# Two chains of a two-layer transformer block on one core: other places for their vector steps

## The reference, cut to what matters

```python
x = x + conv1(ln_c(x))        # window attention: 12 heads over each row of 16 tokens
u = ln_t(tokens(x))
h = u + attention(rms_norm(u, norm1_w), w_qkv, w_out)   # causal, 12 heads, 3 kv heads, rotary
moe_in = rms_norm(h, norm2_w)
out = h + moe_ffn(moe_in)     # softmax router, best 2 of 16 experts
x = x + out                   # x + u + attention + experts
```

## Time and profile before

| | |
|---|---|
| median of 3 runs | 1312.66 us (1312.52 to 1313.05) |
| the profiled execution | 1305.51 us, of which its span is 1303.7 us |
| PE busy | 1053.3 us, 81% of the span |
| DVE, ACT, POOL busy | 57%, 37%, 25% |
| PE's granted clock, mean | 0.927 of full speed |
| chain that ended last | PE 43%, DVE 23%, issue 21% |
| part C | about 533 us, 41% of the span |

### The profile page before, as it was taken

How to read it: one execution, slowest core, us unless ns; L and a number is a source line. 1 busy time by engine, 2 the same in 40 slices (tenths; PEclk the granted TensorE clock), 3 DMA queues, 4 the chain that set the end, 5 groups by cost and what they waited for, 6 DMA issues and landing times.

```text
span 1303.7 us, 26152 instructions
## 1 busy us (share of the span) xinstructions
PE 1053.3 (81%) x9573; PEld 812.8 (62%) x9573; DVE 743.5 (57%) x2307; ACT 488.1 (37%) x1221; POOL 320.0 (25%) x516
## 2 busy tenths in 40 slices
PE   4899999999987998658777777777877663999992
PEld 3677776677665455546565656565655453888882
DVE  6677677668653343445657575757576754333334
ACT  1453354354352221224545454545455541211120
POOL 0000000000003700655435344444101211223222
PEclk8999999999998999788998898999998976999997
DMA  9044044044137994000000000000000005888885
GB/s 342 16 138 136 2 137 137 8 128 137 34 103 231 371 421 155 1 1 2 1 2 13 6 5 13 2 17 1 17 1 18 17 17 205 267 297 287 298 290 164
DMA packets 69040, 144.61 MB, mean 111 GB/s; under 512 B 4896, under 2 KB 55360, under 8 KB 66656
## 3 DMA queue, kind: packets, MB, share of 16 engines
q1 hardware_dynamic: 64352, 132.75, 30.3%
q0 software_dynamic: 4608, 10.79, 2.5%
HBM read 97.22 MB, written 46.30 MB: 110 GB/s over the span
## 4 chain that ended last, share of the span: by engine, by line
PE 43%; DVE 23%; issue 21%; ACT 5%; POOL 4%; DMA 3%; POOLq 0%; DVEq 0%; ACTq 0%; SPq 0%
PE bank L1906 5%; PE bank L1769 4%; DVE neg_max L705 4%; PE bank L560 4%; PE bank L605 3%; PE bank L627 3%; PE bank L669 3%; PE bank L799 2%; PE bank L1797 2%; DVE R L678 2%; PE bank L806 2%; DMA R<-in_ffn_gu 2%; PE bank L1856 2%; PE bank L585 2%; DVE R L867 2%
## 5 line engine op out<-in xcount | busy, mean ns | idle before, releaser
L734 ACT ACTIVATE R<-bank,neg_max 128x128 f32<-128x128 f32 (+2 forms) x576 | 187.7, 399 | 146.4 <-DVE neg_max L705 125.2
L1040 POOL TENSOR_SCALAR R<-cf,ids_rel 128x128 bf16<-128x128 f32 x256 | 168.2, 674 | 0.3
L705 DVE TENSOR_REDUCE neg_max<-bank 128x2 f32<-128x352 f32 (+2 forms) x216 | 129.6, 609 | 64.7 <-PE bank L588 59.7
L605 PE MATMUL bank<-cf,R 128*128 128x128 f32 x864 | 137.7, 283 | 22.3 <-ACT R L734 12.2
L605 PEld LDWEIGHTS bank<-cf,R 128*128 128x128 f32 x864 | 96.6, 144 | 41.5 <-ACT R L734 25.8
L992 POOL TENSOR_TENSOR rstd<-mean_var,cf 128x2 f32<-128x2 f32 x24 | 4.7, 194 | 474.3 <-DVE mean_var L862 474.3
L757 ACT ACTIVATE R<-bank 128x1024 bf16<-128x1024 bf16 x72 | 71.1, 1020 | 80.1 <-PE bank L560 77.7
L1769 PE MATMUL bank<-R 64*116 64x256 f32 (+1 forms) x512 | 97.5, 398 | 0.0
L560 PE MATMUL bank<-cb,R 128*128 128x128 bf16 x1008 | 75.6, 243 | 24.8 <-DVE R L545 24.7
L560 PEld LDWEIGHTS bank<-cb,R 128*128 128x128 bf16 x1008 | 70.0, 111 | 33.8 <-DVE R L545 23.8
L1684 DVE TENSOR_TENSOR R<-R,bank 128x384 f32<-128x384 f32 x48 | 26.6, 554 | 109.5 <-ACT R L1218 106.7
(11 more groups left out here) (251 smaller groups left out, 1997.6 us busy)
## 6 DMA issues: line engine op xcount, KB each, us to landing
R<-in_ffn_w SPq DMA_DIRECT2D x48, 864.0 KB, 5.4
sorted_x<-cmp SPq DMA_DIRECT2D x8, 4128.0 KB, 15.8
R<-in_ffn_gu SPq DMA_DIRECT2D x16, 1392.0 KB, 19.3
R<-in_ffn_dn SPq DMA_DIRECT2D x16, 768.0 KB, 16.4
xs_words<-sorted_x SPq DMA_DIRECT2D x48, 129.0 KB
R<-token_y SPq DMA_DIRECT2D x8, 384.0 KB, 6.4
rows<-R SPq DMA_DIRECT2D x8, 224.0 KB, 2.3
out_x<-x_all SPq DMA_DIRECT2D x16, 96.0 KB, 2.5
```

The source lines that it names most:

```text
L605: ins = nc.tensor.transpose(PT[u % 2][:, at + g * P:at + (g + 1) * P], probs[:, u % 3, g * kw + c0:g * kw + c0 + P], ident)
L705: nc.vector.tensor_reduce(neg_max[:, u % 4, 0:g], score_bank(a, u)[:, 0:g * kw].rearrange("p (g k) -> p g k", g=g), AX, ALU.max, negate=Tr ...
L734: ins = nc.scalar.activation(probs[:, u % 3, g * kw:(g + 1) * kw], score_bank(a, u)[:, g * kw:(g + 1) * kw], ACT.Exp, bias=neg_max[:, u % ...
L1040: ins = nc.gpsimd.tensor_scalar(comb_s[:, t, j, :], cst("iota_tok"), ids_rel[:, j:j + 1], None, ALU.is_equal)
```

## The change

The counts of matmuls and of DVE's attention steps stay. What moves:

- PE's combination matmuls run behind the scores of groups 1, 2 and 3 of the window (30, 30 and 36) instead of groups 0 to 3 (24 each). `causal_qkv` runs behind score 1 instead of score 0. `w_head` and `m_head` stand one group later.
- DVE in the window: `m_rows` behind the first maximum (it was at group 5), `combine` at 3 (was 4), `w_norm` at 5 (was 6) and ahead of its split step, the split steps one group later each.
- DVE in the causal half: the router's steps one or two groups earlier, ahead of the split's; `weights` and `sorted_rows` behind the whole attention and the first two copies of the next q and k.
- u is no longer added to x in `normed`. `causal_sums` adds the projection to u, signals, and adds u to x.
- ACT's `router` one group earlier. PE's `m_head` has a new wait for the variance of image m + 3.

```diff
-                    before[5] = lambda: router(i - 1)
+                    before[4] = lambda: router(i - 1)
...
                 u_ready()
-                link(nc.vector.tensor_tensor(image_x(m), image_x(m), image_u(m), ALU.add))
...
                 await_(dve, CAUSAL, "proj", m, 1)
-                link.inc(nc.vector.tensor_tensor(image_x(m), image_x(m), two(M0[:, 0:2 * C]), ALU.add))
                 link(nc.vector.tensor_tensor(image_u(m), image_u(m), two(M0[:, 0:2 * C]), ALU.add))
                 u_ready()
+                link(nc.vector.tensor_tensor(image_x(m), image_x(m), image_u(m), ALU.add))
...
                 between = {k: [] for k in range(12)}
+                if i >= 1:
+                    between[0].append(lambda: m_rows(i - 1))
+                if i + 2 < B:
+                    between[3].append(lambda: combine(i + 2))
+                    between[5].append(lambda: w_norm(i + 2))
                 if i >= 0:
                     between[1].append(lambda: rotate(i, 0))
                     between[2].append(lambda: rotate(i, 1))
-                    for k, n in ((3, 0), (4, 1), (5, 2), (6, 3), (7, 4), (8, 5)):
+                    for k, n in ((4, 0), (5, 1), (6, 2), (7, 3), (8, 4), (8, 5)):
                         between[k].append(split[n])
-                if i >= 1:
-                    between[5].append(lambda: m_rows(i - 1))
-                if i + 2 < B:
-                    between[4].append(lambda: combine(i + 2))
-                    between[6].append(lambda: w_norm(i + 2))
...
-                for k, n in ((5, 0), (6, 1), (7, 2), (8, 3), (9, 4), (10, 5)):
+                m = i - 1
+                if i >= 1:
+                    between[1].append(lambda: highest_logit(m))
+                    between[4].append(lambda: probabilities(m))
+                    between[5].append(highest)
+                    between[6].append(strike)
+                    between[7].append(lambda: masks(m))
+                    between[7].append(lambda: earlier(m))
+                for k, n in ((3, 0), (4, 1), (5, 2), (8, 3), (9, 4), (10, 5)):
                     between[k] += split[n:n + 1]
...
                 run(copies[:2])
+                if i >= 1:
+                    weights(m)
+                    sorted_rows(m)
...
                 pe.wait_ge(s("c_mr"), m + 1)
+                if m + 3 < B:
+                    pe.wait_ge(s("w_var"), m + 4)
...
-                n = 2 * NPAIR // 4
+                n = 2 * NPAIR // 3
...
-                    if k == 0 and i >= 0:
+                    if k == 1 and i >= 0:
                         causal_qkv(i)
                     if i + 2 < B:
-                        c_comb(i + 2, k * n, (k + 1) * n)
-                for k in range(4):
+                        c_comb(i + 2, (k - 1) * n, k * n if k < 3 else 2 * NPAIR)
+                for k in range(1, 4):
                     extra[k] = lambda k=k: piece(k)
                 if i + 2 < B:
-                    extra[(6, "transposed")] = lambda: w_head(i + 2)
+                    extra[(7, "transposed")] = lambda: w_head(i + 2)
                 if i >= 1:
-                    extra[(7, "transposed")] = lambda: m_head(i - 1)
+                    extra[(8, "transposed")] = lambda: m_head(i - 1)
```

10 lines of the change are left out of this document (removed).

## The result

| | before | change |
|---|---|---|
| time, median of 4 runs | 1312.59 us (1312.27 to 1313.05) | 1269.24 us (1268.68 to 1274.69) |
| ratio to before, 95% interval | | 0.9685 (0.966 to 0.971) |
| profiled run; its span | 1305.51; 1303.7 us | 1268.68; 1266.9 us |
| mean granted clock of PE | 0.927 | 0.939 |

The change is faster by 43 us. A later measurement, beside other runs of before, gave 1269.90 us (1266.82 to 1271.36) against 1313.88, ratio 0.9658 (0.9633 to 0.9683).

What follows compares the result with a forecast made beforehand. PE waits 4.24 us for DVE's late normalisation in the window; DVE bounds the causal half. Terms sum to -31.0 us, with 6.0 clock charge -25.0: 1280.5 profiled, 1287.7 median, range 1278 to 1303.

Steps and rivals of the forecast that it cites:

- The window half: From T, the window's first score matmul, to the causal q and k places: 4.8 us less in turns 2 to 5.
- Places at T + 23.5: Places of the causal q and k ready 23.5 us after the window's first score matmul, instead of T + 28.3.
- The landing: Router's indirect scatter from POOL: lands 1.6 us after its last issue's end, so m_rows starts at T + 7.0.
- The charge: PE's clock may be down when the window's places come: 1.0 us added for each of six windows, 6.0 together.
- The causal half: Rest of a turn, turns 1 to 5: 1.6 us less each, bounds 0.4 and 2.1.
- Turn 6's window: Window without combination matmuls to cover the scatter: 3.5 us more, places at 1008.2.
- Turn 7 and the end: Router rows after the last normalisations: PE gets them 1.5 us later, and 1.7 more after the last turn.
- The base: Forecast starts from the profiled 1305.51 us and adds 7.15 us, the median's distance above the profiled run.
- The clock stays down: Rival: clock down from the window's second wait and at causal halves' ends, 2.5 us per window; 1296.7 us, chance 0.15.
- A new wait on ACT: Rival: ACT's odd-probability copies come late, windows give 2.5 instead of 4.8 us in six turns; 1301.5 us, chance 0.12.
- The scatter decides: Rival: the scatter lands 5.8 us after its issue, holding m_rows to T + 10.3; 1319.5 us, chance 0.08.
- Does not do what it says: Rival: slots reached so late that PE stands at T; at most 0.5 us per turn, counted within the forecast.

Runs made afterwards that it cites:

- kept_busy: Before plus unread matmuls where PE waits: twelve ahead of L785's wait, six ahead of the masks' wait, nothing moved; 1295.85 us, ratio 0.979 to 0.992.
- change_again: The change measured once more, unaltered, beside other runs of before; 1269.90 us, ratio 0.9658.
- row_behind_rotation: The change with m_rows, the router's row, behind both rotations instead of ahead of the second maximum; 1263.39 us, ratio 0.960 to 0.966.

## Why the prediction was right and wrong

**The window half was right**, step by step. Slots at T - 0.2: the cast ends at 704.43, T - 0.35. m_rows at T + 7.0: 711.99, T + 7.2. w_norm done at T + 17.6: 722.57, T + 17.8. w_head reached at T + 19.5: 724.43, T + 19.65. The wait for denominators 1.0: 0.99. PE's waits 0.7, 1.6 and 1.7: 0.94, 1.26 and 1.44. Places at T + 23.5: 728.10, T + 23.3. The gains of turns 0, 1 and 2 to 5 were forecast as 3.6, 4.3 and 4.8; they are 3.9, 4.9 and 4.9 in the mean (28.16 to 23.27).

**The landing.** From the end of the last issue (709.22 + 0.96) to m_rows it is 1.8 us, nearer to the 1.6 of the earlier trace rows. It lies between that and the estimate of 2.3 worked out from the Trainium skill (DMA: Bandwidth & Descriptors, Anatomy of one DMA, SWDGE path). In turns 2 to 5 little hung on it: where the row stands behind the rotations and waits for nothing, a window is 0.85 us shorter (23.27 to 22.42).

**The clock was the failed step**, twice: in the windows I charged for it, and in the causal halves I had no term for it. The charge reads "I charge 1.0 us for each of six windows". I reasoned that three waits of 0.7 to 1.7 us might take PE's clock down as one of 4.2 did. They do not: the windows of turns 0 to 5 are at 0.99 or 1.00, against 0.87 to 0.94 in before. The charge of 6.0 us should have been nothing. The working for the places went by DVE's busy time, which holds no PE clock, so nothing was to be added on that account either. Turn 6's window, without combination matmuls, is at 0.77 (before 0.81), but its length came out within 0.5 us of the sum without a charge. My price was misread besides: 5.11 less 3.67 us is the difference between 1.00 and a mean of 0.64, not "between the levels". By kept_busy 1.7 of the 4.9 us (28.16 to 26.48) could be had from the clock alone, so the old window's loss was partly PE at half speed behind its wait.

**The causal half was mis-sized for the same reason**, and this is the larger part. Forecast 1.6 us per turn, bounds 0.4 and 2.1; measured 3.02 in the mean (38.96 to 35.94). Against kept_busy, where the dip at the end of the half is filled, it is 37.31 to 35.94, 1.4 us; against before's own turn 4, at 1.00, it is 37.22 to 36.06, 1.2: the order was worth a little less than what I gave it. The rest, 1.65 us per turn by kept_busy, is the clock that came back at the end of the half, which had no term. It was to be read in the profile of before: the causal half of turn 4 ran at 1.00 in 37.22 us and the others at 0.91 to 0.96 in 38.50 to 39.96. I used for it only to say that turns differ by the clock, and not to ask what the change would do to it. Together with turn 0's causal half (1.9 less, forecast 0.4; kept_busy, which leaves that half's order alone, already has 1.4 of it) this is 8.6 us. The Trainium skill (TensorE: Matmul & The Clock Gate, Part 1: The HAM clock gate) says that a PE that is little busy is gated down. kept_busy agrees: with the two places filled, its causal half of turn 2 goes from 0.91 to 1.00. What my text left open, which way the new mix of waits goes, the change's own profile settles: 0.99 and 1.00 in the windows of turns 0 to 5, 0.95 to 1.00 in the causal halves.

**The ends.** Turn 6's window 3.5 more: 4.0. Turn 7 and the end: the last wait grew from 3.93 to 5.73 us, 1.8 where I had 1.7. From T6 to the last row 6.4 more was forecast and 7.85 came.

**The base.** I carried over that the median of before lies 7.15 us above its profiled run. In the change it is 0.56, in change_again the median is 1.5 below. Outside the changed part, where the code is the same, the profiled run of before has 739.5 us (1303.7 less 564.18), the change 743.1 and all other kernels 743.2 to 748.9. So the profiled run of before was a short one by 3.6 to 9.4 us, in stretches that the change doesn't touch; with one profile of before, that such a gap belongs to the run and not to the kernel is likely and not shown. Since sum and base were both taken from before this did not move the forecast. It makes up 3.6 of the 6.6 us between the difference of the spans (36.8) and that of the medians (43.4).

The account of the miss of 18.4 us: 6.0 of clock charge, 8.6 in the causal halves, 0.8 net from the other terms of the part (the windows 1.2 and the way to the first turn 1.25 better, turn -1 0.3 and the end 1.45 worse). With the 31.0 of the sum without clock the last two make up the 40.4 that the part lost; 3.0 are between the profiled part and the medians and stay unassigned.

**The rivals.** *The clock stays down:* in turns 0 to 5 the opposite came. *A new wait on ACT:* 0.94 and 1.26 us, 2.2 together where the forecast had 2.3. *The scatter decides:* it landed as in the row. *Does not do what it says:* it does.

## What to carry to other kernels

Where the clock column of before varies between like stretches, it is a term of the sum with its own sign: compare the stretch at the higher clock with the others, and give the difference back if the change removes the idle time ahead of it. Ask also where in the stretch the dip falls. At the end of before's causal half it cost up to 2.3 us (39.56 against 37.22). In the change's, 13 to 10 us ahead of the end, where DVE is the bound, it cost nothing while the half's clock was 0.95, and 1.3 us at 0.91 in row_behind_rotation. Filling PE's idle time with matmuls that nobody reads is a cheap way to measure that term before any reordering. A step that is moved late is paid for at the ends of the loop, where the work that covered it is missing, so move it by turn.

## What the runs showed of the hardware

A wait of 0.98 us and one of 1.10 us that ended 1.9 us later stood ahead of half speed in turn 2 of before (3.59 us for 32 matmuls of 128 x 128), and the same pair ahead of full speed in turn 4 (1.96 us). Over all profiles such a pair was followed by half speed in 12 of 15 halves; where the first wait was missing, none of 55 had it there. In the window of the change three waits of 0.94 to 1.44 us left the clock at 1.00.

Identical code takes either of two lengths. Turn -1 took 42.92 us in the change and 45.77 in change_again, the same kernel. Ten of the profiled kernels have the same code there: eight took 42.90 to 42.92 us and two 45.74 and 45.77. Windows view of the change, then of change_again, some 14 us after the turn's start:

```profile
561.00:576.00 15.00, 9.82 (x70) 6.83 (x69) 6.09 (x19) 4.05 (x10) 9.28 (x18) 1.00 0.00 1
```

```profile
560.00:575.00 15.00, 12.08 (x72) 8.24 (x65) 4.45 (x12) 4.19 (x11) 9.03 (x17) 0.77 0.00 1
```

The same work, at a granted clock of 1.00 or 0.77. The causal half has such a pair as well: 36.07 us at 0.95 and 37.34 at 0.91 in row_behind_rotation. So one profiled run is good for a stretch to about 3 us. The runs of one kernel lie 3 to 11 us apart here (17 in kept_busy, 0.8 in the first four of before); several stretches of that kind would make such a scatter, which no run shows.

DVE's copy L766 at the window's head started when POOL's issue of an indirect DMA ended, in the 17 windows where the two met (T + 0.54 to 0.71, against T + 0.20 to 0.29 in 38 others).
